# Attention's turns written out on every engine, with waits on constants, in a four-layer transformer block

## What is computed

```
x = x + moe(x)                       # layer 0: 8 experts, the best 2 of each token, and shared ones
x = x + attention(x, bias = MLP of the relative position)     # layer 1
x = x + attention(x, bias = fside[16,1024,1024], masked keys) # layer 2
x = x + attention(x, bias = MLP of the relative position)     # layer 3

attention: q = LN(x) Wq (16 heads of 64), one k and one v for all heads, one null key in front,
           sim = q k^T + bias, causal mask, softmax, times v, times Wout, layer norm
```

## Time and profile before

| | us |
|---|---|
| median of 3 runs (2221.52 to 2223.3) | 2221.59 |
| the profiled execution | 2221.87 |
| its span | 2220.1 |

### The profile page before, as it was taken

The page is one execution under the profiler, slowest core; times in us unless marked ns, Lnnn a source line. Parts: engine busy times, 40 slices in busy tenths (PEclk is TensorE's granted clock), DMA queues, the critical chain, the costliest instruction groups (busy, mean ns, idle before and its releaser), DMA issues. The chain is left out here.

```text
span 2220.1 us, 48620 instructions
## 1 busy us (share of the span) xinstructions
PE 1971.5 (89%) x12082; PEld 1439.7 (65%) x12082; DVE 1708.9 (77%) x4092; ACT 1339.0 (60%) x2911; POOL 1067.6 (48%) x1307
## 2 busy tenths in 40 slices
PE   5999586999999998689999999986795999999988
PEld 4888463666666667566666666665563666666668
DVE  4777877788887785757788787858577888888857
ACT  2222665677776674246677666644564777777754
POOL 0443213566765562405566656524023666766643
PEclk8999698899999999798999999998796999999999
DMA  3631068233333343286787777752366334433333
GB/s 118 206 101 41 28 211 280 91 115 114 117 121 106 114 162 112 77 306 201 226 245 244 238 231 231 236 178 77 101 230 193 105 122 122 128 124 114 114 115 115
DMA packets 248203, 338.94 MB, mean 153 GB/s; under 512 B 28838, under 2 KB 154924, under 8 KB 248012
## 3 DMA queue, kind: packets, MB, share of 16 engines
q1 hardware_dynamic: 248012, 336.87, 47.8%
HBM read 250.62 MB, written 102.91 MB: 159 GB/s over the span
## 5 line engine op out<-in xcount | busy, mean ns | idle before, releaser
L1687 POOL TENSOR_SCALAR at_row<-at_row,at_inv 128x769 f32<-128x769 f32 (+7 forms) x384 | 697.9, 1818 | 381.2 <-DVE at_inv L1849 372.9
L1894 ACT ACTIVATE at_row<-at_row,at_nmax 128x769 f32<-128x769 f32 (+7 forms) x768 | 594.7, 774 | 279.4 <-DVE at_nmax L1868 272.3
L1868 DVE CUSTOM_DVE_ANT_0 at_row<-at_s,bias,at_row 128x768 f32<-128x768 f32 (+7 forms) x768 | 610.1, 809 | 81.0 <-PE at_s L1797 39.3
L1809 PE MATMUL at_t<-ident,at_row 128*128 128x128 f32 x3456 | 532.0, 281 | 8.3 <-DVE at_pt L1698 6.5
L1809 PEld LDWEIGHTS at_t<-ident,at_row 128*128 128x128 f32 x3456 | 391.6, 142 | 217.1 <-issue 167.4
L1796 PE MATMUL at_s<-k_hh,q_hl 128*128 128x512 f32 (+3 forms) x1152 | 464.1, 403 | 47.9 <-SPq L1754 23.3
L1824 PE MATMUL at_o<-at_pt,v 128*64 128x256 f32 (+3 forms) x2688 | 460.8, 459 | 1.7 <-DVE at_pt L1698 1.7
L1797 PE MATMUL at_s<-k_lp,q_h 65*128 65x512 f32 (+3 forms) x1152 | 394.6, 354 | 0.0
L1889 ACT ACTIVATE at_pt<-at_t 128x512 f32<-128x512 f32 (+2 forms) x576 | 307.8, 535 | 100.7 <-PE at_t L1809 96.3
L1698 DVE COPY at_pt<-at_t 128x384 f32<-128x384 f32 (+3 forms) x576 | 279.5, 485 | 113.1 <-PE at_t L1809 110.8
L1687 DVE TENSOR_SCALAR at_row<-at_row,at_inv 128x769 f32<-128x769 f32 (+7 forms) x384 | 285.8, 744 | 1.7 <-issue 0.6
(11 more groups left out here) (249 smaller groups left out, 2834.0 us busy)
## 6 DMA issues: line engine op xcount, KB each, us to landing
q_dram<-o_in SPq DMA_DIRECT2D x76, 512.0 KB, 3.8
bias<-bands_dram SPq DMA_DIRECT2D x64, 512.0 KB, 5.8
q_hl<-q_dram SPq DMA_DIRECT2D x96, 256.0 KB, 4.0
q_hl<-q_dram SPq DMA_DIRECT2D x192, 128.0 KB, 3.0
bands_dram<-brow_dram SPq DMA_DIRECT2D x2, 8192.0 KB, 32.8
bias<-corners_dram SPq DMA_DIRECT2D x256, 64.0 KB, 3.4
bias<-in_fside SPq DMA_DIRECT2D x32, 448.0 KB, 3.6
q_h<-q_dram SPq DMA_DIRECT2D x48, 256.0 KB, 4.6
```

The source lines that it names most:

```text
L1687: return eng.tensor_scalar(cells(u), cells(u), inv[:, u % RING:u % RING + 1], None, ALU.mult)
L1809: last = eng.transpose(t_ps[m % NTR][:, c * P:(c + 1) * P], weights(u)[:, here:here + P], t["ident"][:])
L1868: eng.tensor_tensor_reduce(out=weights(u), in0=s_ps[u % 2][:, 0:width], in1=bt[:, lo:lo + width], scale=-1.0, scalar=null_cell(u)[:, 0:1], ...
L1894: eng.activation(cells(u), cells(u), ACT.Exp, scale=-1.0, bias=nmax[:, i:i + 1], accum_out=rsum[:, i:i + 1]).then_inc(s["exp"], 1)
```

## The change

The hardware loops of `attend` become Python loops, so that each turn is written out on each engine, and the turn is a number wherever it was a register. Waits compare with constants, and the DMAs' addresses are constants. All nine increments of `gate` in `attend` go, with the semaphore's name. The order of all steps stays, as do all loads, stores and arithmetic. The two conditions on `out_weights` and `low_weights` are rewritten so that these still fall in turn 3.

```diff
@@ run_halves
     for half in range(B):
-        with eng.Fori(0, turns - 1) as turn:
+        for turn in range(turns if half < B - 1 else turns - 1):
             steps(half, turn, late, size + late, lambda n, per: True)
-        if half < B - 1:
-            steps(half, turns - 1, late, size + late, lambda n, per: True)
     steps(B - 1, turns - 1, late, size + late, peeled(B * turns - 1))
@@ attend, SP: store, queries, row_bias (the same line goes in each)
                     place.wait(eng, "out", g + 1)
-                    eng.sem_inc(s["gate"], 1)
@@ attend, SP
-                with eng.Fori(1, TURNS) as turn:
-                    loads(place(0, turn), False)
-                for half in range(1, B):
-                    with eng.Fori(0, TURNS) as turn:
-                        loads(place(half, turn), False)
+                for turn in range(1, B * TURNS):
+                    loads(place(turn // TURNS, turn % TURNS), False)
@@ ScalarE; GpSimd has the same with low_weights, n % 6 == 2 and 14 <= n < 38
-                    if turn.known() and 0 <= turn.turn < TURNS and turn.half < B - 1 and n % 6 == 0 and 12 <= n < 36:
+                    if turn.turn == TURNS - 1 and turn.half < B - 1 and n % 6 == 0 and 12 <= n < 36:
                         out_weights(n // 6 - 2)
```

More of the change, by code:

```diff
@@ L1645, in attend @@
                  ev_d=NPC // 2, pv=NGRP, out=NGRP)
-    names = list(marks) + ["q0", "q1", "gate", "wo_in", "wo_hi", "wo_lo", "o0", "o1"] + [f"bias{n}" for n in range(NBIAS)]
+    names = list(marks) + ["q0", "q1", "wo_in", "wo_hi", "wo_lo", "o0", "o1"] + [f"bias{n}" for n in range(NBIAS)]
     def slot_loads(n):
@@ L1952, in step @@
                 def step(turn, n, has):
-                    if turn.known() and 0 <= turn.turn < TURNS and turn.half < B - 1 and n % 6 == 2 and 14 <= n < 38:
+                    if turn.turn == TURNS - 1 and turn.half < B - 1 and n % 6 == 2 and 14 <= n < 38:
                         low_weights(n // 6 - 2)
```

## The result

| | before | after |
|---|---|---|
| median | 2222.45 us (2221.52 to 2224.15) | 2186.23 us (2184.73 to 2187.03) |
| span of the profiled execution | 2220.1 | 2185.2 |
| attention of layers 1, 2, 3 | 440.29, 455.00, 428.08 | 423.99, 441.04, 425.01 |

The kernel is 36.2 us faster: a ratio of 0.9835, with an interval from 0.9818 to 0.9852. The forecast was 2179 us, with a range from 2173 to 2192. The span of the profiled execution fell by 34.9 us: by layer, the windows give 16.30, 13.96 and 3.07 us, and 1.57 us lie elsewhere.

What follows compares the result with a forecast made beforehand. The prediction took TensorE's 53.53 us turn as the floor, with VectorE's long branches disturbing layers 1 and 3 and SP bounding layer 2. 14.0 + 3.0 + 26.0 = 43.0 us off 2221.87 gave 2179 us, range 2173 to 2192.

Steps and rivals of the forecast that it cites:

- Branches on VectorE: Layers 1 and 3: long branches back of about 2.9 us go, gaining 14.0 us and 3.0 us.
- The six disturbed turns: Turns 1, 2, 5, 6 of layer 1 and 5, 6 of layer 3, expected at 53.5 to 53.8 us.
- third rival: The change does nothing measurable, long stops being luck of the run: 2221.6 us; chance 3%.
- SP in layer 2: SP's list bounds layer 2's attention; written out, SP stops being the bound: gain 26.0 us, between 15.0 and 29.9.
- the prices of its list: SP in layer 2, written out: 0.94 us a bias pair, 0.635 a query load, 42.4 us a turn.
- the worst case: Layer 2: seven turns each keep 2.07 us and turn 0 its 0.38, 14.9 us staying; gain 15.0 us.
- the residual of 0.5 us a turn: Layer 2: excess taken to stay after the change, 3.9 us with turn 0, which was the nearest row.
- first rival: Layer 2 is held by its data (ring room, landing), not SP: 2204.6 us, anything up to 2190; chance 10%.
- The sign by which I wanted to know it: Layer 2 turns staying above 55 us while SP waits would make the prediction wrong and show the data-bound case.
- Register operations and increments of the other engines: Compute engines: register operations and `gate` increments hide behind TensorE, no further gain.
- Written-out code: More code in written-out turns, straight code being prefetched: cost nothing.
- second rival: Written-out turns stall TensorE or VectorE at block ends, 1.41 us a stop: 2229.4 us; chance 5%.

Runs made afterwards that it cites:

- VectorE alone: The kernel before with VectorE's loops over turns written out and nothing else: 2204.19 us, ratio 0.9926.

## Why the prediction was right, and where it was off

*Branches on VectorE.* Predicted 14.0 us in layer 1 and 3.0 in layer 3; the windows give 16.3 and 3.07. VectorE alone gives 15.9 and 2.95. The six disturbed turns are at 53.53 us, as said, and line 188 is gone. Two terms of layer 1 were small misses. The 0.27 us that I left in each of turns 1 and 2 went as well, and with it the 0.28 of turn 3. And turn 0, which I had not counted, fell from 51.49 to 50.09 us. Nothing in the change is seen to set that part; it goes with the clock. The turn's first 15 us run at a granted clock of 0.61 in the kernel before and of 0.69 in after, as the rows below show, and in the two other profiles of after it is 0.65 and 0.62, with a turn of 50.55 and 51.02 us.

```profile
392.08:407.08 15.00, 14.33 (x55) 11.34 (x54) 11.38 (x29) 8.73 (x20) 6.93 (x10) 0.61 0.13 33
...
390.64:405.64 15.00, 13.89 (x59) 10.84 (x58) 12.69 (x30) 9.87 (x22) 8.21 (x10) 0.69 0.21 50
```

The third rival (stops by luck of the run) falls: the same six turns were long with SP alone written out, and none was with 64 increments ahead.

*SP in layer 2.* That SP was the bound, and the prices of its list, were right: SP waits 11.4 us a turn where I had said 8 to 11. The gain was mis-sized: 26.0 us taken, 14.0 in this profile, 17.9 and 18.9 in the two others of after (437.06 and 436.12). The 14.0 us lie below the 15.0 that I had called the worst case. The step that failed is the residual of 0.5 us a turn. It measured 1.7 to 2.0 us a turn (55.18 to 55.50 us against 53.53) in turns 1 to 4 and 6, and 2.4 in the mean of the seven, since the two stretches at the lower clock add to it; in the two other profiles the mean is 1.8 and 1.6. I had named both of its causes and added them up in neither place: in the first rival that units 0 to 4 may be issued only 4 or 5 units ahead, and in the step itself that unit 8's bias stands behind six query loads. They are one chain. With 1.0 us for the room, which no row showed, and the prices of the earlier trace rows, five pairs (4.7), six query loads (3.8), two stores (0.9) and unit 8's own first load (0.5) make 10.9 us. With the 3.5 us of landing that I had, the bias is there at 14.4 us, where VectorE wants it at 14.55: on time, with no slack at all. With the 5.3 us measured in after it is there at 16.2, 1.7 us late. In turn 2 itself it landed at 16.8 us, 5.7 after its issue; the addition came 2.4 us late, and the turn was 1.8 us longer, so that the chain regains some 0.6 us behind it. Where that comes from was not looked into. I chose turn 0 as the nearest row for what stays, but turn 0 is the one turn without such a head, since its first units have the whole ring.

*Landing.* I carried over 3.5 us for the landing of a corner, the last 128 columns of a unit's bias. In after it is 5.3 us in layer 2 (median; 3.4 before), while the mean load of the queues rose from 0.78 to 0.84. It is 5.0 at a load of 0.85 in another profile of after, 4.7 at 0.86 with TensorE's loops back, and 4.5 at 0.81 with the ring that runs on, which moves more bytes a second (253 GB/s in the layer against 243). So the mean load alone doesn't set it; that the bursts behind the wait for room do was not tested by itself. The row that shows it in after, turns 1 to 7 of layer 2:

```profile
bias<-corners_dram SPq DMA_DIRECT2D x222, 64.0 KB, 5.3
```

That the queues carry it at 85% was right (0.85 of turn 2), but it left out that each load may take longer to land.

*The first rival* held more truth than its 10%. Its own number, 2190 to 2204.6 us, was not reached, but its mechanism decides what is left of layer 2. The sign by which I wanted to know it, turns above 55 us while SP waits, is there: by that sign my account of layer 2 was wrong, though the time of the kernel fell into the range. The kernel lies between forecast and rival: about two thirds of the predicted gain of layer 2 came in the mean of the three profiles, (14.0 + 17.9 + 18.9) / 3 = 16.9 of 26.0.

*Register operations and increments of the other engines* at nothing: right, as far as 2 us can be told. *Written-out code* at nothing: no such stop was found on TensorE or VectorE, whose turns stand at the floor in layers 1 and 3, and the second rival is out; its effect on SP's issues was not foreseen.

*The sum.* 16.30 + 13.96 + 3.07 + 1.57 elsewhere = 34.90 us in the span, against 43.0. The 8.1 us missing are layer 2 (-12.0), lessened by layer 1 (+2.3), layer 3 (+0.1) and what lies elsewhere (+1.6), for which no step of the prediction has a cause. That the time fell well inside the range owes something to these 4 us.

## What to carry to other kernels

When an issuing engine is found to be the bound, giving it time only helps up to the next thing that it may not pass. Add up the chain that follows each such point (room, the loads queued ahead of the first late one, landing under the new load) before taking a value near zero for what stays. A ring of buffers that begins anew with each turn puts a wait of its own at every head; letting it run on was worth 12 us here (2184.57 to 2172.46), nearly as much as the branches of VectorE. And of a loop whose branch back costs 2.9 us, ask first where its code lies: moving it was worth 11 us in the one execution of that kernel, where writing it out was worth 15.6.

## What was not expected of the hardware

- A branch back of VectorE took 2.8 to 3.05 us or 0.3 us depending on 64 instructions placed ahead of it, in a loop that was otherwise the same.
- While a block of TensorE's code is fetched (16.4 KB, about 1 us), an SP DMA issue that falls into it takes up to 1.0 us longer (1.46 instead of 0.43 us in the fence above; 0.6 us in the mean of 20).
- The same 64 KB loads landed in 3.4 us (median) with the slow issue, in 4.6 to 5.3 with the fast one in five kernels with the old ring and order, and in 4.5 with the ring that runs on.
